# A layer norm's scale moved into VectorE's product and its bias into narrow matmuls, in place of ScalarE's affine step

## The chip, the cores and the metric

The kernel runs on one core of one Trainium2 chip. The metric is the device time of one execution in microseconds (us), and the median of several executions is compared.

## What is computed

Two sequences of 1024 tokens with 128 channels go through a recurrent mixing layer and a norm, then through six layers of local attention (16 heads of 64, windows of 32) and feed-forward, and a last norm. The change lies in the feed-forward, whose hidden width is 341, twice (a and gate). All of it is fp32. Cut to what matters:

```python
def ffn_layer(x, g, bln, W1, b1, W2, b2):
    mu = x.mean(-1, keepdims=True)
    var = ((x - mu) ** 2).mean(-1, keepdims=True)
    xn = (x - mu) / jnp.sqrt(var + 1e-05) * g + bln
    hg = xn @ W1 + b1
    a, gate = jnp.split(hg, 2, -1)
    return a * jax.nn.gelu(gate, approximate=False) @ W2 + b2
for i in range(DEPTH):
    x = attn_layer(shift_tokens(x), Wqkv[i], q_scale[i], k_scale[i], Wo[i]) + x
    x = ffn_layer(shift_tokens(x), ln_g[i], ln_b[i], W1[i], b1[i], W2[i], b2[i]) + x
```

## The kernel before

The first 320 us or so are the mixing layer, which the change does not touch. After it comes the stream: 96 blocks of 128 tokens, 16 blocks to a layer, one after the other through all six layers. `x` is kept with its channels on the partitions and the tokens along the free axis, and every stage of a block is a function of the block's number `n`. The feed-forward stages work on a pair of blocks, 256 tokens, numbered `m`; a layer has eight pairs (`BLOCK_PAIRS`).

The order on each engine is written by hand. Each engine has a `turn`, a list of stages with lags, and `stream` runs it once for each `n`: `at(2, turn_k)` means that turn `n` does `turn_k` for block `n - 2`, and `pair(5, norm_x)` does `norm_x` for a pair in every other turn, once its second block is five turns back. So a pair of turns makes one period. The engines meet in semaphores only, one for each kind of step (`Signal`), and `after(n)` is the count that tells that block or pair `n` has it.

The attention part of a block: TensorE projects q and k in four products of 512 columns (`project_qk`, L1370) and v in two (`project_v`, L1375); ScalarE squares q and k (`square`, L1603), VectorE multiplies them with the rotary tables (`rotate`, L1770) and sums the squares (`norms`, L1776), ScalarE makes the inverse norms, GpSimd adds the turned halves (L1308) and applies the norms (L1314). TensorE transposes q and k (L1383), multiplies them in small tiles (`scores`, L1418), VectorE subtracts the peak and sums (L1782 to L1798), GpSimd normalizes the probabilities (L1332) and multiplies the rotary tables by the gains (L1297, `gains`, which `rotate` of the block waits for). VectorE turns the probabilities in blocks of 32 (`turn_p`, L1804), the SP queue places them and shifted values with DMAs, and TensorE makes the outputs in small tiles (`outputs`, L1443).

The feed-forward part of a pair: `project_o` (L1460, eight products of 256 columns into `FF_BANK`) waits for `o_T` and for `x_ready` of the pair before. `add_attention` on VectorE (L1809) adds `x` and writes `xm`; `centres` (L1467) subtracts the mean with a matmul, ScalarE squares (L1650), `variances` (L1471) takes the mean of the squares, and `inverse_sigma` on ScalarE (L1655, L1657) makes `rstd`, spread over all partitions. VectorE's `norm_x` (L1814) multiplies the centred tile by `rstd` into `xn`, and ScalarE's `affine` (L1663) makes `xn_T` of it with the scale and the bias of the layer, one number a channel and so one a partition. TensorE's `up` (L1477) makes the gate columns and then the a columns from `xn_T` in three parts of 128, 128 and 85 (`FF_PARTS`). ScalarE's `gelu` (L1670) adds b1's gate part, VectorE's `gated` (L1822) adds b1's a part and multiplies, `down` (L1501) is the second product, and `add_ffn` (L1843) writes the new `x` and sets `x_ready`.

The piece of TensorE's turn in which the change puts its matmuls:

```python
            at(0, project_qk, 3)
            at(0, project_v, 0)
            pair(4, project_o, 0)
            pair(4, project_o, 1)
            at(3, outputs, 0)
```

After the last turn the stages that are left stand in a list of their own, with the last norm and the stores of the result between them. The weights of a layer (2.4 MB) are loaded one layer ahead by the SP queue, behind the DMAs of the seventh block of the layer in work.

## Time and profile before

| what | value |
|---|---|
| median of 3 runs | 1926.08 us (1924.15 to 1927.91) |
| profiled execution, span from its first to its last instruction | 1924.9 us |
| profiled execution, its own time | not on the page; the runs' median is 1.2 us above its span |
| instructions in the span | 72907 |
| busy share of the span: PE, PEld, DVE, ACT, POOL | 91%, 62%, 81%, 59%, 65% |
| TensorE's granted clock, mean | 0.958 of full speed |
| stream | from about 320 us to the end, 96 blocks |

PE is TensorE's matmuls, PEld its weight loads, DVE is VectorE, ACT is ScalarE, POOL is GpSimd. In the profile an fp32 matmul of the program appears as two records, each with a weight load of its own; the transposes appear as one. A start that follows the one before by less than that one's duration is a pipelined start, so what an instruction costs in a row of its kind is the distance of starts. In the timelines "x16" merges sixteen records, and what stands in brackets is idle time before them and what ended it. The rows that the prediction uses stand in a section of their own below.

### The profile page before, as it was taken

How to read it: one execution, taken by the hardware profiler on the slowest of the kernel's cores; microseconds unless marked ns; L12 is line 12 of the kernel's file. 1: busy time of each engine (PE TensorE's matmuls, PEld its weight loads, DVE VectorE, ACT ScalarE, POOL GpSimd, SP SyncE). 2: the span in 40 equal slices, each digit the busy share in tenths (PEclk: the TensorE clock that was granted, in tenths of full speed). 3: DMA queues.
4: the chain of work that ended last, by engine and by line, in shares of the span. 5: the costliest groups of instructions: out<-in, count | busy, mean ns of one | idle time of the engine just before them, and what ended most of it. 6: DMA issues, size and time to landing. Idle time of an engine off the chain costs nothing.

```text
span 1924.9 us, 72907 instructions
## 1 busy us (share of the span) xinstructions
PE 1751.1 (91%) x31158; PEld 1185.3 (62%) x31158; DVE 1550.0 (81%) x2150; ACT 1138.0 (59%) x2221; POOL 1259.8 (65%) x981
## 2 busy tenths in 40 slices
PE   7577876899999989999899999899998999999985
PEld 2144553466666666667666767666666676666663
DVE  6599957788888878888888888788887888888853
ACT  5523223557676747676667676667675667676742
POOL 3476743777777767777667777677776777777730
PEclk9699977999999989999999999999998999999986
DMA  4534201222222232222322222322223222222220
GB/s 97 127 53 51 29 3 70 58 67 70 69 73 68 72 104 79 63 75 70 112 66 79 69 73 83 103 62 77 69 72 109 69 68 79 63 76 67 70 61 26
DMA packets 68257, 137.27 MB, mean 71 GB/s; under 512 B 17952, under 2 KB 23520, under 8 KB 66912
## 3 DMA queue, kind: packets, MB, share of 16 engines
q1 hardware_dynamic: 67936, 132.62, 27.0%
q8 instruction: 246, 4.03, 0.9%
q14 instruction: 75, 0.61, 0.1%
HBM read 29.79 MB, written 2.10 MB: 17 GB/s over the span
## 4 chain that ended last, share of the span: by engine, by line
PE 40%; DVE 22%; issue 11%; POOL 9%; DMA 7%; ACT 4%; SPq 2%; DVEq 0%; ACTq 0%; POOLq 0%
PE bank L1460 9%; PE bank L1370 6%; PE bank L1443 6%; POOL rot L1308 5%; DMA v_shift<-v_tok 5%; DVE rot L1770 5%; PE bank L1418 5%; PE bank L1501 3%; PE bank L1375 3%; PE bank L1477 3%; DVE total L1796 2%; DVE rnorm L1776 2%; POOL probs L1332 2%; DVE probs L1789 2%; DMA p_T<-p_blocks 1%
## 5 line engine op out<-in xcount | busy, mean ns | idle before, releaser
L1770 DVE TENSOR_TENSOR rot<-bank,gains 128x1024 f32<-128x1024 f32 x384 | 462.3, 1206 | 158.8 <-ACT squares L1603 142.8
L1314 POOL TENSOR_TENSOR rot<-rot,rnorm 128x1024 f32<-128x1024 f32 x192 | 361.0, 1901 | 319.3 <-ACT rnorm L1613 317.1
L1308 POOL TENSOR_TENSOR rot<-rot 128x512 f32<-128x512 f32 x384 | 480.6, 1274 | 6.9 <-DVE rot L1770 6.9
L1370 PE MATMUL bank<-wqkv,x 128*128 128x512 f32 x768 | 404.9, 612 | 10.5 <-issue 5.0
L1603 ACT ACTIVATE squares<-bank 128x512 f32<-128x512 f32 x384 | 232.8, 606 | 256.5 <-PE bank L1370 255.9
L1332 POOL TENSOR_TENSOR probs<-probs,total 128x1024 f32<-128x1024 f32 x96 | 182.7, 1903 | 125.3 <-DVE total L1798 125.3
L1644 ACT ACTIVATE o_T<-bank 128x512 f32<-128x512 f32 x192 | 104.2, 598 | 254.2 <-PE bank L1443 254.2
L1776 DVE TENSOR_REDUCE rnorm<-squares 128x16 f32<-128x1024 f32 x192 | 233.0, 1214 | 2.8
L1443 PE MATMUL bank<-p_T,v_shift 64*64 64x32 f32 x6144 | 194.7, 223 | 26.6 <-DMA p_T<-p_blocks 21.9
L1443 PEld LDWEIGHTS bank<-p_T,v_shift 64*64 64x64 f32 x6144 | 169.2, 138 | 79.1 <-issue 49.6
L1383 PEld LDWEIGHTS bank<-st_ident,rot 128*128 128x128 f32 x1536 | 179.9, 143 | 59.9 <-issue 53.6
L1375 PE MATMUL bank<-wqkv,x 128*128 128x512 f32 x384 | 206.6, 621 | 2.7 <-DVE rot L1770 2.7
L1443 PE MATMUL bank<-p_T,v_tok 64*64 64x32 f32 x6144 | 193.3, 222 | 4.4 <-issue 4.4
L1383 PE MATMUL bank<-st_ident,rot 128*128 128x128 f32 x1536 | 194.0, 275 | 0.0
L1460 PE MATMUL bank<-o_T,wo 128*128 128x256 f32 x768 | 176.9, 384 | 0.0
L1443 PEld LDWEIGHTS bank<-p_T,v_tok 64*64 64x64 f32 x6144 | 170.5, 139 | 5.5 <-issue 5.4
L1477 PE MATMUL bank<-xn_T,w 128*128 128x256 f32 (+1 forms) x576 | 164.5, 395 | 9.2 <-ACT gate_T L1670 2.2
L1460 PEld LDWEIGHTS bank<-o_T,wo 128*128 128x128 f32 x768 | 146.4, 192 | 42.9 <-issue 22.4
L1418 PE MATMUL bank<-k_T,q_T 64*32 64x64 f32 x12288 | 161.8, 225 | 11.8 <-issue 10.3
L1418 PEld LDWEIGHTS bank<-k_T,q_T 64*32 64x32 f32 x12288 | 140.8, 105 | 39.2 <-issue 33.1
L1477 PEld LDWEIGHTS bank<-xn_T,w 128*128 128x128 f32 (+1 forms) x576 | 97.7, 182 | 99.2 <-DVE ff_T L1822 45.5
L1370 PEld LDWEIGHTS bank<-wqkv,x 128*128 128x128 f32 x768 | 131.6, 191 | 39.1 <-issue 16.2
(196 smaller groups left out, 2849.2 us busy)
## 6 DMA issues: line engine op xcount, KB each, us to landing
p_T<-p_blocks SPq DMA_DIRECT2D x768, 64.0 KB
v_shift<-v_tok SPq DMA_DIRECT2D x96, 384.0 KB, 3.5
v_shift<-v_tok SPq DMA_DIRECT2D x96, 128.0 KB, 3.4
wqkv<-in_wqkv SPq DMA_DIRECT2D x6, 1536.0 KB, 8.0
v_rep_sb<-v_by_step SPq DMA_DIRECT2D x32, 128.0 KB
v_rep<-v_by_step SPq DMA_DIRECT2D x32, 128.0 KB
wo<-in_wo SPq DMA_DIRECT2D x6, 512.0 KB, 8.6
w<-in_w SPq DMA_DIRECT2D x6, 341.0 KB, 8.8
```

The source lines that it names most:

```text
L1308: nc.gpsimd.tensor_tensor(out=out, in0=out, in1=by_head(turned[:, part])[:, :, frm], op=ALU.add).then_inc(rot_added.sem, 1)
L1314: nc.gpsimd.tensor_tensor(out=by_head(qk[u][:, half]), in0=by_head(qk[u][:, half]), in1=rnorm[u][:, AH * i:AH * (i + 1)].unsqueeze(2).to_b ...
L1370: nc.tensor.matmul(QK_BANKS[i][:, :], shifted_tokens(x, n, P), layer_cols(wqkv, n, 3 * INNER, 512 * i, 512), start=True, stop=True).then_i ...
L1375: nc.tensor.matmul(V_BANKS[i][:, :], shifted_tokens(x, n, P), layer_cols(wqkv, n, 3 * INNER, 2 * INNER + 512 * i, 512), start=True, stop=T ...
L1383: mm = nc.tensor.transpose(outs[i // 4][:, P * (i % 4):P * (i % 4 + 1)], source[:, P * i:P * (i + 1)], ident[:, :])
L1418: mm = nc.tensor.matmul(s_banks(n)[p][at:at + WINDOW, 2 * WINDOW * a_:2 * WINDOW * (a_ + 1)], q_T[rows, a_, at:at + WINDOW], k_T[rows, a_, ...
L1443: mm = nc.tensor.matmul(o_banks(n)[g][DH * p:DH * (p + 1), at:at + WINDOW], v[rows, DH * head:DH * (head + 1)], p_T[n % 2][rows, turn_, he ...
L1460: mm = nc.tensor.matmul(ff_bank(m)[:, 0:PT], layer_cols(wo, n, INNER, C * i, C), o_T[:, i, :], start=(i == 0), stop=(i == PAIRS - 1))
L1477: mm = nc.tensor.matmul(ff_bank(m)[0:size, PT * j:PT * (j + 1)], layer_cols(w1, PAIR * m, 2 * FF, at + f0, size), xn_T[:, :], start=True, ...
L1603: nc.scalar.activation(squares[:, 512 * i:512 * (i + 1)], QK_BANKS[i][:, :], ACT.Square).then_inc(squared.sem, 1)
L1770: nc.vector.tensor_tensor(both, src.unsqueeze(1).to_broadcast([P, 2, 8, DH]), pair_of_gains.unsqueeze(2).to_broadcast([P, 2, 8, DH]), ALU. ...
L1776: nc.vector.reduce_sum(rnorm[n % 2][:, AH * h:AH * (h + 1)], by_head(squares[:, INNER * h:INNER * (h + 1)]), AX).then_inc(ss_made.sem, 1)
```

## The change

`norm_x` on VectorE becomes one instruction with two multiplications, (centred x scale) x rstd, and writes `xn_T` itself. The bias of the norm goes around the large product: once a layer, `shift_up` on TensorE multiplies the layer's W1, six column parts of it, with the column of the norm's bias, into six unused columns of `FF_BANK`, ahead of `project_o` of the layer's first pair. `shift_b1` on VectorE adds b1 to them with four small instructions ahead of that pair's `xm` and writes `b1_shifted`, which `gelu` and `gated` use in place of b1. ScalarE's `affine` is gone, and with it the tile `xn` and its semaphore. The waits that went with it are moved: the first logarithm of `inverse_sigma` waits for `xnT_made` of the pair before, and `norm_x` waits for the a product of the pair before, which has read `xn_T`.

```diff
+        def shift_up(m):
+
+            layer = m // BLOCK_PAIRS
+            for i, (f0, size) in enumerate(FF_PARTS):
+                for half in range(2):
+                    nc.tensor.matmul(FF_BANK[0:size, PT + len(FF_PARTS) * half + i:PT + len(FF_PARTS) * half + i + 1],
+                                     layer_cols(w1, PAIR * m, 2 * FF, FF * half + f0, size),
+                                     norm_gb[:, layer + DEPTH:layer + DEPTH + 1], start=True, stop=True)
+
         def project_o(m, h):
...
+            if h == 0 and m % BLOCK_PAIRS == 0:
+                shift_up(m)
             for i in range(PAIRS // 2 * h, PAIRS // 2 * (h + 1)):
...
         def inverse_sigma(m):
             act.wait_ge(var_product.sem, var_product.after(m))
-            act.wait_ge(x_normed.sem, x_normed.after(m - 1))
+            act.wait_ge(xnT_made.sem, xnT_made.after(m - 1))
...
-        def affine(m):
-            act.wait_ge(x_normed.sem, x_normed.after(m))
-            act.wait_ge(a_product.sem, a_product.after(m - 1))
-            layer = m // BLOCK_PAIRS
-            nc.scalar.activation(xn_T[:, :], xn[:, :], ACT.Identity, scale=norm_gb[:, layer:layer + 1],
-                                 bias=norm_gb[:, layer + DEPTH:layer + DEPTH + 1]).then_inc(xnT_made.sem, 1)
-
         def gelu(m, i):
-            size, col = FF_PARTS[i][1], (m // BLOCK_PAIRS) * 2 * len(FF_PARTS) + len(FF_PARTS) + i
+            size, layer, col = FF_PARTS[i][1], m // BLOCK_PAIRS, len(FF_PARTS) + i
+            act.wait_ge(b1_made.sem, layer + 1)
...
-                                 bias=b1[0:size, col:col + 1]).then_inc(gate_made.sem, 1)
+                                 bias=b1_shifted[layer % 2][0:size, col:col + 1]).then_inc(gate_made.sem, 1)
...
+        def shift_b1(layer):
+
+            cols = 2 * len(FF_PARTS)
+            for size, parts in ((P, (0, 1)), (FF_PARTS[-1][1], (2,))):
+                for half in range(2):
+                    part = slice(len(FF_PARTS) * half + parts[0], len(FF_PARTS) * half + parts[-1] + 1)
+                    add = nc.vector.tensor_tensor(b1_shifted[layer % 2][0:size, part], FF_BANK[0:size, PT:PT + cols][:, part],
+                                                  b1[0:size, cols * layer:cols * (layer + 1)][:, part], ALU.add)
+            add.then_inc(b1_made.sem, 1)
+
         def add_attention(m):
             dve.wait_ge(y_product.sem, y_product.after(m))
+            if m % BLOCK_PAIRS == 0:
+                shift_b1(m // BLOCK_PAIRS)
...
         def norm_x(m):
             dve.wait_ge(rstd_made.sem, rstd_made.after(m))
-            dve.wait_ge(xnT_made.sem, xnT_made.after(m - 1))
-            nc.vector.tensor_tensor(xn[:, :], ff_bank(m)[:, 0:PT], rstd[:, :], ALU.mult).then_inc(x_normed.sem, 1)
+            dve.wait_ge(a_product.sem, a_product.after(m - 1))
+            layer = m // BLOCK_PAIRS
+            nc.vector.scalar_tensor_tensor(out=xn_T[:, :], in0=ff_bank(m)[:, 0:PT], scalar=norm_gb[:, layer:layer + 1], in1=rstd[:, :],
+                                           op0=ALU.mult, op1=ALU.mult).then_inc(xnT_made.sem, 1)
 
         def gated(m, i):
...
+            dve.wait_ge(b1_made.sem, layer + 1)
...
-                                           scalar=b1[0:size, col:col + 1], in1=gate_T[0:size, i, :],
+                                           scalar=b1_shifted[layer % 2][0:size, i:i + 1], in1=gate_T[0:size, i, :],
```

TensorE in the turn in which the first pair of the second layer has its `project_o` (`w` is W1 or W2, `bank` a PSUM bank). Before:

```order
L1370 MATMUL bank<-wqkv,x 128x512
L1501 MATMUL bank<-ff_T,w_0 128x256 x3
L1370 MATMUL bank<-wqkv,x 128x512
L1375 MATMUL bank<-wqkv,x 128x512
L1460 MATMUL bank<-o_T,wo 128x256 x8
L1443 MATMUL bank<-p_T,v_shift 64x32 x4
L1443 MATMUL bank<-p_T,v_tok 64x32 x4
```

And now:

```order
L1372 MATMUL bank<-wqkv,x 128x512
L1514 MATMUL bank<-ff_T,w_0 128x256 x3
L1372 MATMUL bank<-wqkv,x 128x512
L1377 MATMUL bank<-wqkv,x 128x512
L1455 MATMUL bank<-norm_gb,w_1 128x1 x4
L1455 MATMUL bank<-norm_gb,w_1 85x1 x2
L1473 MATMUL bank<-o_T,wo 128x256 x8
L1445 MATMUL bank<-p_T,v_shift 64x32 x4
L1445 MATMUL bank<-p_T,v_tok 64x32 x4
```

The six narrow matmuls stand between `project_v` and `project_o`; the rest is as before, with other line numbers.

VectorE at the first pair of the first layer, from the last `rot` of one turn to the second of the next. Before:

```order
L1770 TENSOR_TENSOR rot<-bank,gains 128x2x512
L1809 TENSOR_TENSOR xm<-bank,x 64x256 x2
L1776 TENSOR_REDUCE rnorm<-squares 128x16
L1804 STREAM_TRANSPOSE p_blocks<-probs 128x1024
L1770 TENSOR_TENSOR rot<-bank,gains 128x2x512
L1814 TENSOR_TENSOR xn<-bank,rstd 128x256
L1770 TENSOR_TENSOR rot<-bank,gains 128x2x512
```

And now (`b_shifted` is `b1_shifted`):

```order
L1773 TENSOR_TENSOR rot<-bank,gains 128x2x512
L1815 TENSOR_TENSOR b_shifted<-bank,b 128x2 x2
L1815 TENSOR_TENSOR b_shifted<-bank,b 85x1 x2
L1824 TENSOR_TENSOR xm<-bank,x 64x256 x2
L1779 TENSOR_REDUCE rnorm<-squares 128x16
L1807 STREAM_TRANSPOSE p_blocks<-probs 128x1024
L1773 TENSOR_TENSOR rot<-bank,gains 128x2x512
L1830 SCALAR_TENSOR_TENSOR xn_T<-bank,norm_gb,rstd 128x256
L1773 TENSOR_TENSOR rot<-bank,gains 128x2x512
```

The four small adds stand ahead of `xm`, and the product that wrote `xn` is a SCALAR_TENSOR_TENSOR that writes `xn_T`.

## Rows read from the trace of the kernel before

**Rows 1.** The page's head and its part 1 (busy us, share, instructions)
```profile
span 1924.9 us, 72907 instructions
...
PE 1751.1 (91%) x31158; PEld 1185.3 (62%) x31158; DVE 1550.0 (81%) x2150; ACT 1138.0 (59%) x2221; POOL 1259.8 (65%) x981
```

**Rows 2.** Windows of three pairs: us; busy PE, PEld, DVE, ACT, POOL; clock; DMA
```profile
1103.22:1134.24 31.02, 30.91 (x617) 21.45 (x611) 26.85 (x35) 21.17 (x41) 22.70 (x17) 1.00 0.27 70
1009.70:1040.90 31.20, 31.09 (x613) 21.78 (x610) 27.16 (x35) 21.17 (x41) 23.02 (x19) 1.00 0.26 70
1196.70:1235.40 38.70, 33.28 (x618) 23.39 (x611) 26.97 (x35) 21.54 (x41) 22.85 (x18) 0.91 0.43 128
```

**Rows 3.** Chain of waits, 1095 to 1165: start us, us, what
```profile
1107.72 0.65 ACT squares L1603
...
1109.53 0.41 DVE xn L1814
...
1117.22 1.06 POOL probs L1332
```

**Rows 4.** Timeline of PE, 1100 to 1136: start us, us, work
```profile
1103.22 0.70 PE L1467 MATMUL bank<-xm,centring 128*128 128x256 f32 x2
...
1104.62 1.91 PE L1383 MATMUL bank<-st_ident,rot 128*128 128x128 f32 x16
1106.36 1.02 PE L1370 MATMUL bank<-wqkv,x 128*128 128x512 f32 x2
...
1110.47 1.13 PE L1370 MATMUL bank<-wqkv,x 128*128 128x512 f32 x2
1111.43 1.03 PE L1477 MATMUL bank<-xn_T,w 128*128 128x256 f32 x4
...
1124.55 1.13 PE L1370 MATMUL bank<-wqkv,x 128*128 128x512 f32 x2
1125.51 1.46 PE L1501 MATMUL bank<-ff_T,w 128*128 128x256 f32 x6
...
1128.55 3.69 PE L1460 MATMUL bank<-o_T,wo 128*128 128x256 f32 x16
1132.17 0.32 PE L1443 MATMUL bank<-p_T,v_shift 64*64 64x32 f32 x8
...
1134.24 0.70 PE L1467 MATMUL bank<-xm,centring 128*128 128x256 f32 x2
```

**Rows 5.** Timeline of DVE, the same stretch
```profile
1102.18 0.86 DVE L1809 TENSOR_TENSOR xm<-bank,x 64x256 f32<-64x256 f32 x2
...
1133.32 0.86 DVE L1809 TENSOR_TENSOR xm<-bank,x 64x256 f32<-64x256 f32 x2
```

**Rows 6.** Part 5 (busy us, mean ns | idle before), weight loads
```profile
L1460 PEld LDWEIGHTS bank<-o_T,wo 128*128 128x128 f32 x768 | 146.4, 192 | 42.9 <-issue 22.4
```

**Rows 7.** Timeline of PE, first pair of the first layer
```profile
395.70 1.02 PE L1467 MATMUL bank<-xm,centring 128*128 128x256 f32 x2 [1.34 <-DVE xm L1809]
```

**Rows 8.** Groups by line and form, DVE and ACT, 300 to 1900
```profile
L1789 DVE TENSOR_TENSOR probs<-bank,peak 128x512 f32<-128x512 f32 x192 | 122.7, 680 | 0.0
...
L1822 DVE SCALAR_TENSOR_TENSOR ff_T<-bank,b,gate_T 128x256 f32<-128x256 f32 x94 | 41.2, 480 | 71.7 <-PE bank L1477 71.7
...
L1814 DVE TENSOR_TENSOR xn<-bank,rstd 128x256 f32<-128x256 f32 x48 | 19.9, 415 | 8.0 <-ACT rstd L1657 8.0
...
L1663 ACT ACTIVATE xn_T<-xn,norm_gb 128x256 f32<-128x256 f32 x48 | 28.1, 586 | 1.0 <-DVE xn L1814 1.0
```

**Rows 9.** Timeline of ACT, 1100 to 1136
```profile
1111.69 0.60 ACT L1603 ACTIVATE squares<-bank 128x512 f32<-128x512 f32 x1 [0.73 <-PE bank L1370]
```

**Rows 10.** Waits of the weight loads, 400 to 1800: us in total, times, longest
```profile
PEld bank L1477 <- ACT xn_T L1663: 9.7, 38, 0.4
```

**Rows 11.** Timelines of ACT and PE in the tail
```profile
1896.35 0.58 ACT L1663 ACTIVATE xn_T<-xn,norm_gb 128x256 f32<-128x256 f32 x1
...
1896.60 1.80 PE L1501 MATMUL bank<-ff_T,w 128*128 128x256 f32 x6 [2.66 <-DVE ff_T L1822]
```

More of the change, by code:

```diff
@@ L1125, in build_stream @@
     xm = sb("xm", (P, B, T + 1))
-    cent_sq, rstd, xn, xn_T = (sb(n, (P, PT)) for n in ("cent_sq", "rstd", "xn", "xn_T"))
+    cent_sq, rstd, xn_T = (sb(n, (P, PT)) for n in ("cent_sq", "rstd", "xn_T"))
+    b1_shifted = two("b1_shifted", (P, 2 * len(FF_PARTS)))
     gate_T, ff_T = sb("gate_T", (P, len(FF_PARTS), PT)), sb("ff_T", (P, len(FF_PARTS), PT))
@@ L1149, in build_stream @@
     cent_squared, var_product, var_log, rstd_made = sig("cent_squared"), sig("st_var_product"), sig("var_log"), sig("rstd_made")
-    x_normed, xnT_made = sig("x_normed"), sig("xnT_made")
+    xnT_made = sig("xnT_made")
+    b1_made = sig("b1_made", credit=0)
     gate_product, gate_made, a_product = sig("up_gate_product", per=2), sig("gate_made", per=3), sig("up_a_product", per=2)
@@ L1592, in scalar @@
         for s in (squared, above_floor, rnorm_log, rnorm_made, v_read, qT_made, kT_made, exp_made, oT_made,
-                  cent_squared, var_log, rstd_made, xnT_made, gate_made):
+                  cent_squared, var_log, rstd_made, gate_made):
             act.sem_inc(s.sem, s.credit * s.per)
@@ L1692, in turn @@
             at(1, inverse_norms)
-            pair(5, affine)
             at(0, square, 2)
@@ L1716, in scalar @@
         inverse_sigma(m - 2)
-        affine(m - 2)
         read_q(LAST)
@@ L1727, in scalar @@
         inverse_sigma(m - 1)
-        affine(m - 1)
         read_o(LAST - 1)
@@ L1736, in scalar @@
         final_inverse(0, 0, 12)
-        affine(m)
         gelu_full(m)
@@ L1749, in vector @@
             nc.vector.memset(tile, 0.0).then_inc(cleared.sem, 1)
-        for s in (x_ready, rotated, ss_made, peak_made, shifted, total_made, p_turned, xm_made, x_normed, ff_made):
+        for s in (x_ready, rotated, ss_made, peak_made, shifted, total_made, p_turned, xm_made, xnT_made, ff_made):
             dve.sem_inc(s.sem, s.credit * s.per)
@@ L1812, in norm_x @@
             dve.wait_ge(rstd_made.sem, rstd_made.after(m))
-            dve.wait_ge(xnT_made.sem, xnT_made.after(m - 1))
-            nc.vector.tensor_tensor(xn[:, :], ff_bank(m)[:, 0:PT], rstd[:, :], ALU.mult).then_inc(x_normed.sem, 1)
+            dve.wait_ge(a_product.sem, a_product.after(m - 1))
+            layer = m // BLOCK_PAIRS
+            nc.vector.scalar_tensor_tensor(out=xn_T[:, :], in0=ff_bank(m)[:, 0:PT], scalar=norm_gb[:, layer:layer + 1], in1=rstd[:, :],
+                                           op0=ALU.mult, op1=ALU.mult).then_inc(xnT_made.sem, 1)
         def gated(m, i):
-            size, col = FF_PARTS[i][1], (m // BLOCK_PAIRS) * 2 * len(FF_PARTS) + i
+            size, layer = FF_PARTS[i][1], m // BLOCK_PAIRS
+            dve.wait_ge(b1_made.sem, layer + 1)
             dve.wait_ge(a_product.sem, a_product.after(m, 1 + i // 2))
```

## The prediction

> **What bounds the kernel now.** I read the page first: TensorE is busy 91% of the span of 1924.9 us [rows 1]. That share is a mean over stages, so next came the windows [rows 2]: a steady pair of blocks takes 31.02 us, another 31.20 us, with TensorE busy in all but 0.1 us of it and its clock granted in full (1.00, the level of 2.4 GHz), and a pair in which a layer's weights are loaded takes 38.70 us, where TensorE stands still for 5.4 us. Then the chain of waits over one pair [rows 3]. It goes through ScalarE's squares, VectorE's stretch from `rot` over `xn` to `total`, and GpSimd's `probs` and `rot`, before it comes back to TensorE. So two cycles run side by side: TensorE's own work, and one that passes through VectorE and GpSimd. Which of them ends last decides what each edit is worth.
>
> The timelines of that pair show how close they are. TensorE [rows 4]: `project_o` (from 1128.55, 3.62 us long) is followed at once by `outputs` (1132.17), and `centres` starts at 1134.24. VectorE [rows 5]: `xm`, which `centres` waits for, ends at 1133.32 + 0.86 = 1134.18, only 0.06 us before. One pair earlier it ends at 1103.04 and `centres` starts at 1103.22, 0.18 us later. Taken in the same way, 19 of 44 pairs have the small distance (0.05 to 0.08 us: VectorE ends last) and 25 the large one (0.15 to 0.28 us: TensorE ends last).
>
> **The narrow matmuls (six a layer).** Where the order rows have eight `project_o` matmuls, the trace has sixteen records, so an fp32 matmul runs as two, and six make twelve: eight with 128 weight columns, four with 85. With one moving column each, the weight load sets their time. The nearest row is the transposes [rows 4]: 16 records from 1104.62 to 1106.36, each with a load of 128 columns of its own, 0.109 us apart. Twelve, with the narrower ones scaled, are 0.109 x (8 + 4 x 85/128) = 1.2 us a layer. Lower bound: `outputs` runs 128 records in 2.07 us on four quadrants, 0.065 us for a 64-column load and its matmul in a quadrant, so 12 x 0.065 = 0.8 us. Upper bound: 0.192 us, what a 128-column load lasts alone [rows 6], 2.3 us. I take 1.2, since the transposes have the same loads in the same close order. The Trainium skill (TensorE: Matmul & The Clock Gate, LDWEIGHTS) gives a load's time as its columns / 1.2 in ns; the twelve would be 1.1 us by it, an estimate, and the sum 0.5 us smaller.
>
> All of it stands on TensorE between `project_v` and `project_o`, where there is no hole, and `outputs`, the reads by ScalarE behind it and so both cycles come after it. Five layers pay in full, 6.0 us. The first pays less: there TensorE waited 1.34 us for `xm` [rows 7], since VectorE was late with its own work. The product for `xm` comes 1.2 us later, still inside that work, and only what VectorE itself adds ahead of `xm` is left, some 0.3 us. Sum: **+6.3 us** (bounds 4.3 and 11.8).
>
> **VectorE's product.** A TENSOR_TENSOR of 0.415 us becomes a SCALAR_TENSOR_TENSOR of 128x256 with an operand in PSUM, and that costs 0.480 us in `gated` [rows 8]: 0.065 us x 48 = 3.1 us if all of it were on the path. It stands in the stretch of [rows 3], whose lateness comes back through GpSimd's `gains` to VectorE's next `rot`. In the 19 close pairs it shows; in the 25 others it fits into the 0.1 us by which TensorE is later: 19 x 0.065 = **+1.2 us** (0 to 3.1).
>
> **VectorE's four small adds a layer.** A tensor_tensor takes 0.415 us at 256 columns and 0.680 at 512 [rows 8]; drawn down to one or two columns that is 0.15 us, so four are at most 0.6 us. Behind them in the queue stand `xm`, the second `rnorm` and the next `p_blocks`. The product that they wait for now ends 1.2 us later, just as VectorE is done with its last `rot`. From there 0.1 + 0.6 + 0.86 us to the end of `xm` are 1.56 us, while TensorE is in `outputs` for 2.07 us: **0 us** (0.6 x 6 = 3.6 us if that cover were gone). `p_blocks` comes 0.6 us later where all of TensorE comes 1.2 us later.
>
> **ScalarE's affine step.** 48 x 0.586 = 28.1 us of busy time go [rows 8]. In the pair it is followed by 0.73 us of idle time until TensorE's product for the third square [rows 9], so that square starts no earlier: **0 us**. `xn_T` itself is ready earlier, straight from VectorE. The weight loads of the gate product did wait for it, 9.7 us in 38 times [rows 10], but its matmuls not visibly: from `project_qk` 2 to the gate product are 0.96 us, and exactly as much from `project_qk` 2 to `down` in the other half [rows 4], whose `ff_T` had been ready for over 1 us. So 0 here too (at best -9.7 us).
>
> **Waits.** The gelu and `gated` now also wait for `b1_made`, which is set a block ahead of them; the first logarithm and the product now wait for things of the pair before that were done some 10 us earlier: 0. Behind the gelu on ScalarE stand the reads of `o_T`, and so TensorE, but what it waits for is not later than before. The queues of SP and GpSimd issue what they did.
>
> **The tail.** For the last pair the affine step ran from 1896.35 to 1896.93, while TensorE was in `down` of the pair before, from 1896.60 to 1898.40 [rows 11]. Taking it out gives nothing. The longer product stands ahead of the last part of `ff_T`, for which that `down` had waited: +0.1 us.
>
> **Sum:** 6.3 + 1.2 + 0.1 = +7.6 us, on the profiled span 1932.5 us. The page gives no other time for that execution; the median of the three runs, 1926.08 us, is 1.2 us above the span, so I add to the median: **1933.7 us**, 0.4% slower. A difference of 0.2% (3.9 us) is about what a measurement of this kernel can tell from none.
>
> **Rivals.**
> 1. *VectorE becomes the bound.* Every pair pays 0.065 us and every layer the adds: 6.3 + 3.1 + 3.6 = +13.0 us, 1939.1 us. For it: the 19 close pairs. Against: the 0.1 us in hand in the other 25, and the 0.5 us over the adds. Chance 0.14.
> 2. *The narrow matmuls and their loads take turns.* Each record then costs a load of 0.192 us [rows 6] and a short matmul, for which I take 0.2 us (eight of `outputs` end within 0.32 us [rows 4]): 12 x 6 x 0.39 = 28 us, with the rest +29 us, 1955 us. Against: the sixteen records of `project_o` take 3.62 us, 0.226 each, and would take 0.4 if the loads were not beside them. Chance 0.03. By the Trainium skill (TensorE: Matmul & The Clock Gate, The mechanism) a load overlaps a running matmul only when it goes to another row group, and these all take the full height, so that section speaks for this rival; here the trace does not agree with it, by the 0.226 us.
> 3. *The narrow matmuls are absorbed,* in the stalls of the weight loads (38.70 against 31.1 us [rows 2]) and in the 0.2 us that `project_o` is slower than its columns. Then 1.3 us are left: 1927.4 us, no change. Against: the stalls come two blocks behind these matmuls, and the transfers that cause them are released by TensorE's `outputs`, so they move with it. Chance 0.08.
> 4. *TensorE gets back the wait for `xn_T`.* 7.6 - 9.7 = -2.1 us: 1924.0 us, no change. For it: [rows 10]. Against: the 0.96 us in both halves. Chance 0.05.
> 5. *Faster, because ScalarE was on the path.* This decides from the point at which ScalarE has no idle time ahead of the third square: then a pair gains the affine step's own time, 28.1 us in all, less 7.6: 1905.6 us. For it: the chain passes through ScalarE's squares. Against: the 0.73 us [rows 9], and no piece of the chain in this pair is the affine step. Chance 0.05, with the cases in which a part of it joins rival 4.
>
> **How the numbers follow.** The forecast has the 0.65 that is left. Slower by over 0.2%: the forecast and rivals 1 and 2, 0.82, less 0.02 for a forecast that a measurement places lower: 0.80. Within 0.2%: rivals 3 and 4 and that 0.02: 0.15. Faster: 0.05. The range leaves out rivals 2, 4 and 5, 0.13. Its foot is rival 3, 1927.0; its head, 1941.0, is rival 1 with a third of the way from 6.3 to 11.8 for the loads.
>
> **What would show it.** Right: narrow matmuls 0.1 us apart and 1.2 us more from `project_v` to `project_o` in the first pair of layers two to six; the product at 0.48 us; ScalarE 28 us less busy and idle for as much longer ahead of `squares`; `xm` ready some 0.5 us before `centres` in a layer's first pair; other pairs at 31.0 to 31.2 us. Wrong: ordinary pairs above 31.3 us (rival 1), 0.3 us or more from one narrow matmul to the next (rival 2), pairs with stalls shorter than 38 us (rival 3), ordinary pairs under 31.0 us (rivals 4 and 5).

## The result, and the profile after

The changed kernel takes 1936.31 us (median of 8 runs, 1928.77 to 1941.79), the kernel before 1923.42 us in the same session (8 runs, 1918.60 to 1929.32). The ratio is 1.0057 with a 95% interval of 1.0037 to 1.0078: slower by 11.0 us, between 7.1 and 15.0. The two medians alone are 12.9 us apart, which lies inside the same interval. The forecast was +7.6 us and slower. Differences below are ratios to the kernel before, turned into us with 1923.42; the quotient of two medians can be another one, by up to 3.4 us. One of the 12 executions of run 10 took 2077.15 us, at a granted clock of 0.82 where the others had 0.95 to 0.96, and is left out of its ratio.

The profiled execution of the change was the fastest of its eight, 1928.77 us, with a span of 1926.8. So its page shows where single pieces went, but not the whole difference. The head and part 1 of its page, against [rows 1]:

```profile
span 1926.8 us, 73122 instructions
...
PE 1752.9 (91%) x31230; PEld 1190.3 (62%) x31230; DVE 1553.7 (81%) x2174; ACT 1114.2 (58%) x2173; POOL 1260.3 (65%) x981
```

TensorE has 72 records more (6 x 12), VectorE 24 more, ScalarE 48 fewer. ScalarE is busy for 23.8 us less. The forecast's 28.1 us were the affine step alone; its other groups differ between the two executions as well. What became of that time is in part 5 of the same page, in the row of the squares:

```profile
L1616 ACT ACTIVATE squares<-bank 128x512 f32<-128x512 f32 x384 | 232.6, 606 | 273.6 <-PE bank L1372 273.0
```

On the page of the kernel before, the same group has 256.5 us idle ahead of it. 17.1 of the 23.8 us have turned into waiting for TensorE. In the pair itself, the 0.73 us of [rows 9] are now 1.40 (ScalarE's timeline, 1104 to 1128):

```profile
1109.37 0.60 ACT L1616 ACTIVATE squares<-bank 128x512 f32<-128x512 f32 x1 [1.40 <-PE bank L1372]
```

The windows of three pairs from `centres` to `centres`, with the columns of [rows 2]: an ordinary one, the first of a layer, and one in which a layer's weights are loaded.

```profile
1100.72:1131.98 31.26, 31.09 (x615) 21.76 (x611) 27.23 (x35) 20.67 (x40) 22.98 (x19) 1.00 0.27 70
1131.97:1164.19 32.22, 32.05 (x629) 22.69 (x623) 27.92 (x39) 20.68 (x40) 23.90 (x18) 1.00 0.26 68
1195.38:1235.88 40.50, 34.29 (x617) 23.98 (x611) 27.05 (x35) 21.01 (x40) 22.89 (x18) 0.92 0.41 123
```

From `centres` to `centres`, the first pairs of layers two to six took 31.01, 31.06, 31.27, 31.17 and 31.91 us before, and take 32.64, 32.22, 32.21, 32.20 and 32.21 now: 1.0 us more on average. The shortest ordinary pair is 31.07 us against 31.02, while the mean of the ordinary pairs under 31.45 us (neither the first of a layer nor one in which weights are loaded, and without the tail) is 31.15 against 31.16. The four pairs in which weights are loaded took 38.37 to 40.57 us before and 37.56 to 40.50 now, with no direction in them.

TensorE's timeline where layer one turns over, 385 to 400. The matmuls of `project_v` are followed by the narrow ones and these by `project_o`; it answers to [rows 7]:

```profile
385.38 1.12 PE L1377 MATMUL bank<-wqkv,x 128*128 128x512 f32 x2
386.35 1.25 PE L1455 MATMUL bank<-norm_gb,w 128*128 128x1 f32 x12
387.46 3.70 PE L1473 MATMUL bank<-o_T,wo 128*128 128x256 f32 x16
...
393.56 0.70 PE L1480 MATMUL bank<-xm,centring 128*128 128x256 f32 x2 [0.41 <-DVE xm L1824]
```

Twelve records from 386.35 to 387.46: 1.11 us, 0.093 us each. It is 1.11 and 1.12 us in layers two and three, and 1.19 us (0.099 each) in layers four to six. And the idle time ahead of `centres` fell from 1.34 to 0.41 us, so in this pair most of the added time was taken out of a wait that was there already, as the forecast had it.

The group of the weight loads at that line (count: shortest/median/longest ns, first to last start; forms), then VectorE's groups of the small adds and of the product:

```profile
L1455 PEld LDWEIGHTS bank<-norm_gb,w x72: 155/190/192, 385.9 to 1678.8; 128*128 128x128 f32 x48, 128*85 128x85 f32 x24
```

```profile
L1815 DVE TENSOR_TENSOR b_shifted<-bank,b x24: 143/146/160, 392.4 to 1682.8; 128x2 f32<-128x2 f32 x12, 85x1 f32<-85x1 f32 x12
L1830 DVE SCALAR_TENSOR_TENSOR xn_T<-bank,norm_gb,rstd x48: 450/475/483, 399.9 to 1896.3; 128x256 f32<-128x256 f32 x48
```

A load lasts 190 ns by its own record, yet a load and its matmul come every 93 ns, so these loads overlap each other as well, as far as their records tell. The product is 475 ns (forecast 480, before 415) and an add 146 ns (forecast 150).

VectorE's and TensorE's timelines, 1158 to 1176, in the first pair of layer four. They answer to [rows 4, 5]:

```profile
1161.06 1.16 DVE L1773 TENSOR_TENSOR rot<-bank,gains 128x1024 f32<-128x1024 f32 x1
1162.30 0.35 DVE L1815 TENSOR_TENSOR b_shifted<-bank,b 128x2 f32<-128x2 f32 x4
1162.57 0.87 DVE L1824 TENSOR_TENSOR xm<-bank,x 64x256 f32<-64x256 f32 x2
...
1170.50 0.47 DVE L1830 SCALAR_TENSOR_TENSOR xn_T<-bank,norm_gb,rstd 128x256 f32<-128x256 f32 x1
```

```profile
1158.56 3.70 PE L1473 MATMUL bank<-o_T,wo 128*128 128x256 f32 x16
...
1164.19 0.70 PE L1480 MATMUL bank<-xm,centring 128*128 128x256 f32 x2
```

The four adds overlap and delay `xm` by 0.27 us, not 0.6. `xm` ends at 1163.44 and `centres` starts at 1164.19, with 0.75 us in hand. Forecast were 0.5.

So far each step looks as forecast. One distance does not. In the half of a pair in which `down` is issued, the forecast put the new wait of `gated` at nothing. Here is TensorE's timeline of the kernel before, 1114 to 1133, and that of the change, 1104 to 1128, from the second `project_qk` of the turn to the last a product (`up_a_tail`, 85 weight columns). That product waits for `ff_T`, which VectorE makes with two `gated` steps in a row:

```profile
1120.97 1.02 PE L1370 MATMUL bank<-wqkv,x 128*128 128x512 f32 x2
1122.10 0.66 PE L1477 MATMUL bank<-xn_T,w 128*85 128x256 f32 x2
```

```profile
1118.65 1.02 PE L1372 MATMUL bank<-wqkv,x 128*128 128x512 f32 x2
1119.84 0.66 PE L1490 MATMUL bank<-xn_T,w 128*85 128x256 f32 x2 [0.17 <-DVE ff_T L1840]
```

1.13 us have become 1.19, and TensorE is now shown as waiting 0.17 us for `ff_T`. It waited there before as well: `project_qk` ends at 1120.97 + 1.02 = 1121.99 and the product starts 0.11 us later, too little for the timeline to show. So VectorE's `ff_T` came last at this place already, and anything that delays `gated` reaches TensorE. Over 45 pairs the median went from 1.132 to 1.187 us: 0.055 us a pair, 2.5 us in the span if every pair became longer by as much.

### The profile page after: what moved, and what is told of

Same layout as the page of the kernel before. It is cut to its first block and busy times, and to the rows that moved or that the text cites. A ratio compares the mean times of both kernels' runs of the same rounds, so it can differ in the third digit from the quotient of the medians.

```text
span 1926.8 us, 73122 instructions
## 1 busy us (share of the span) xinstructions
PE 1752.9 (91%) x31230; PEld 1190.3 (62%) x31230; DVE 1553.7 (81%) x2174; ACT 1114.2 (58%) x2173; POOL 1260.3 (65%) x981
```

## The experiments

Two theories went in for the 3.4 us between forecast and result, although the interval of the result (7.1 to 15.0) does not force such a gap. By the first, it is the wait of `gated` for `b1_made`, which is always met but stands as a fourth wait ahead of a step with three. By the second, each part costs somewhat more than forecast: the product in every pair, or the narrow matmuls do, by what they do to the clock or to the weight loads behind them. Each run gives the median of its own kernel; the ratio is to the kernel before, timed on the same chip in the same session (medians 1924.73 to 1925.33 us there).

**1. The wait for `b1_made` once a layer** (against the changed kernel):

```diff
             size, layer = FF_PARTS[i][1], m // BLOCK_PAIRS
-            dve.wait_ge(b1_made.sem, layer + 1)
+            if i == 0 and m % BLOCK_PAIRS == 0:
+                dve.wait_ge(b1_made.sem, layer + 1)
             dve.wait_ge(a_product.sem, a_product.after(m, 1 + i // 2))
```

and the same in the gelu, with `act`.

> The change, with the wait for b1_made taken once a layer (first pair, first part of gelu and of gated) in place of six times a pair. What it computes is unchanged. Seen in the trace of the change: from the second project_qk of a turn to the last a product, TensorE needs 1.19 us where before it needed 1.13, in every pair, and VectorE's ff_T starts 1.11 us after the a product in place of 1.06. Theory A (a fourth wait ahead of gated delays it by 0.05 to 0.06 us each pair, on TensorE's path): the distance returns to 1.13 us and the time is 2 to 3 us below the change. Theory B (the distance comes from the new operand tile or from the state of the run, not from the wait): 1.19 us stays, no difference to the change.

Measured: 1934.11 us (6 runs), ratio 1.0051 (1.0034 to 1.0068), so +9.8 us; and the distance is back at 1.132 us. With the wait gone from all but the layer's first step, the longer distance is gone. The ratio agrees with a gain of 1.2 us over the change, and with none, since the intervals lie over each other.

**2. The change without the shift of b1.** The call of `shift_up`, the adds and the waits for `b1_made` go, and the gelu and `gated` take `b1` as before:

```diff
-            if h == 0 and m % BLOCK_PAIRS == 0:
-                shift_up(m)
...
-            if m % BLOCK_PAIRS == 0:
-                shift_b1(m // BLOCK_PAIRS)
...
-            dve.wait_ge(b1_made.sem, layer + 1)
```

> The change without its narrow matmuls, small adds and b1_made: the norm's bias is left out of the result, b1 is used as it is. It leaves VectorE's longer product and the missing affine step. Theory of the prediction: slower than before by 1.2 us (0 to 3.1), pairs in which VectorE ends last at 31.08 us in place of 31.02, the first pair of a layer like any other (31.1 to 31.3 us, against 32.2 in the change). Rival (ScalarE's freed time is worth something): faster than before by 3 us or more. Rival (the narrow matmuls cost more than their 1.1 us, for instance in later stalls): the change less this one is well over 9 us.

Measured: 1927.84 us (12 runs), ratio 1.0013 (0.9998 to 1.0029), so +2.5 us (-0.4 to 5.6). Its first pairs take 31.1 to 31.4 us but for one of 32.18, and the distance is 1.132 us. What is left of the change in it is the product and the missing affine step. Against run 1, the narrow matmuls and the adds are worth 1.0051 - 1.0013, or 7.3 us, with some 4 us of uncertainty.

**3. The narrow matmuls twice** (against the changed kernel):

```diff
-            for i, (f0, size) in enumerate(FF_PARTS):
+            for i, (f0, size) in list(enumerate(FF_PARTS)) * 2:
                 for half in range(2):
```

> The change with the six narrow matmuls of a layer made twice (the same columns written again). Theory: twelve more records 0.1 us apart, so the first pair of layers two to six takes 33.3 us in place of 32.2, 5 to 6 us in all over the change. Rival (they are taken up by the stalls behind the weight loads): the first pairs grow, the stalled pairs (37.6 to 40.5 us) shrink by as much, no difference to the change.

Measured: 1950.22 us (4 runs), ratio 1.0137 (1.0112 to 1.0161), so +26.4 us, and 15.4 more than the change. Doubling a cost of 5.6 to 7.3 us should add as much again, not twice as much. TensorE's timeline, 1690 to 1706, and the windows on and behind the narrow matmuls of the sixth layer show a part of it:

```profile
1694.83 2.45 PE L1455 MATMUL bank<-norm_gb,w 128*128 128x1 f32 x24
1697.14 5.39 PE L1473 MATMUL bank<-o_T,wo 128*128 128x256 f32 x16
```

```profile
1694.80:1697.90 3.10, 3.10 (x29) 2.99 (x28) 3.07 (x3) 0.98 (x2) 1.66 (x2) 1.00 0.00 0
1697.90:1701.30 3.40, 3.40 (x10) 2.69 (x9) 1.56 (x3) 0.00 (x0) 2.81 (x2) 0.50 0.00 0
```

`project_o` takes 5.39 us in place of 3.70, because the granted clock right behind the 24 narrow records is 0.50, the level of 1.2 GHz. The same happens in layer five (3.41 us from 1435.1), and in no other. In those two layers the first pairs take 35.32 and 35.60 us, in the other three 34.11, 33.41 and 33.41 (35.60 and 34.11 hold a pause of 0.35 and of 0.61 us on TensorE besides, of the kind that the end of the next section describes). Set against 33.41 us, the two clock drops come to 1.9 and 1.8 us. Behind the twelve narrow records of the change every such window has a clock of 1.00:

```profile
1158.50:1162.00 3.50, 3.50 (x19) 3.00 (x18) 3.46 (x4) 0.00 (x0) 1.90 (x2) 1.00 0.02 5
```

**4. The kernel before, with `gated` waiting for its product alone:**

```diff
             dve.wait_ge(a_product.sem, a_product.after(m, 1 + i // 2))
-            dve.wait_ge(gate_made.sem, gate_made.after(m, i + 1))
-            dve.wait_ge(y2_product.sem, y2_product.after(m - 1))
```

> The kernel before, with gated on VectorE waiting for the a product alone; the two other waits are implied by it, since TensorE makes the a product only after the gate tile is made and after the down product of the pair before. Nothing else differs. Theory A (a wait ahead of gated costs some 0.05 us on TensorE's path): from the second project_qk to the last a product 1.02 to 1.08 us in place of 1.13, pairs in which TensorE ends last shorter by as much, 2 to 5 us faster than before. Theory B (waits that are already met cost nothing): 1.13 us, no difference.

Measured: 1926.97 us (12 runs), ratio 1.0004 (0.9987 to 1.0022); the distance is 1.133 us. One wait or three ahead of `gated` is the same, in the distance and, within 4 us, in the time.

**5. The kernel before, without the affine step;** its result lacks the norm's scale and bias, and the product writes `xn_T` itself:

```diff
-            nc.vector.tensor_tensor(xn[:, :], ff_bank(m)[:, 0:PT], rstd[:, :], ALU.mult).then_inc(x_normed.sem, 1)
+            nc.vector.tensor_tensor(xn_T[:, :], ff_bank(m)[:, 0:PT], rstd[:, :], ALU.mult).then_inc(xnT_made.sem, 1)
...
-        affine(m - 2)
```

> The kernel before without ScalarE's affine step: VectorE's product (a TENSOR_TENSOR, as before) writes xn_T itself, and the scale and the bias of the norm are left out of the result. Theory (ScalarE is not on the path): no difference to before, within 0.1%; ScalarE 28 us less busy, idle for as much longer. Rival (part of the freed time, or of TensorE's weight loads that waited for xn_T, comes back): 3 to 10 us faster.

Measured: 1926.73 us (11 runs), ratio 1.0001 (0.9987 to 1.0016). On its page the idle time ahead of `squares` rises from 256.5 to 277.9 us. 28.1 us of busy time gone are worth nothing, within 3 us either way; so rival 4 (9.7 us to be gained) and rival 5 (28.1 us) are out.

**6. The scale alone moved into the product,** with the affine step kept for the bias, the kernel before otherwise:

```diff
-            nc.vector.tensor_tensor(xn[:, :], ff_bank(m)[:, 0:PT], rstd[:, :], ALU.mult).then_inc(x_normed.sem, 1)
+            layer = m // BLOCK_PAIRS
+            nc.vector.scalar_tensor_tensor(out=xn[:, :], in0=ff_bank(m)[:, 0:PT], scalar=norm_gb[:, layer:layer + 1], in1=rstd[:, :],
+                                           op0=ALU.mult, op1=ALU.mult).then_inc(x_normed.sem, 1)
```

> The kernel before with the norm's scale in VectorE's product (SCALAR_TENSOR_TENSOR) and the affine step kept for the bias. Same result. Theory: the product takes 0.475 us in place of 0.415, the pairs in which VectorE ends last take 31.08 us in place of 31.02, about 1 us slower than before (0 to 3), too little to be told from none in the times. Rival (VectorE's extra comes back in every pair): all ordinary pairs 0.06 us longer, 3 us slower.

Measured: 1928.76 us (10 runs), ratio 1.0017 (1.0004 to 1.0030), so +3.3 us (0.8 to 5.8). The shortest pair is 31.07 us, as in the change; the mean of the ordinary pairs is 31.155 us, as before (31.160). The time lies nearer to the product in every pair (3.1 us) than to 19 of 44 (1.2 us), but the interval holds both. The trace lies between: of its 44 pairs, 27 have the small distance from `xm` to `centres` that the forecast counted 19 times in the kernel before (25 of 44 in run 2). 27 x 0.065 = 1.8 us.

**7. The kernel before, with a fourth wait ahead of `gated`,** for a semaphore that has always been raised by then:

```diff
+            dve.wait_ge(gains_made.sem, gains_made.after(2 * m))
             dve.wait_ge(a_product.sem, a_product.after(m, 1 + i // 2))
```

> The kernel before with a fourth wait ahead of gated on VectorE, for a count that was reached long before. Same result. Theory: the distance from the second project_qk to the last a product is 1.19 us in place of 1.13 in every pair; where TensorE ends last the pair is 0.06 us longer, so 1 to 3 us slower than before. Rival (the distance in the change came from something else): 1.13 us, no difference.

Measured: 1931.24 us (12 runs), ratio 1.0030 (1.0016 to 1.0044), so +5.8 us (3.1 to 8.5). The distance is 1.187 us, the same as that of the change (TensorE's timeline):

```profile
1119.24 1.02 PE L1370 MATMUL bank<-wqkv,x 128*128 128x512 f32 x2
1120.43 0.66 PE L1477 MATMUL bank<-xn_T,w 128*85 128x256 f32 x2 [0.17 <-DVE ff_T L1823]
```

No data and no work differ here. A wait that is met on arrival costs time, and the row that names `ff_T` as what TensorE waits for comes from it. How it reaches the pairs is less simple. Windows of the same two neighbouring pairs, in the kernel before and then here:

```profile
978.69:1009.72 31.03, 30.92 (x617) 21.34 (x611) 26.82 (x35) 21.17 (x41) 22.65 (x17) 1.00 0.27 71
1009.72:1040.92 31.20, 31.09 (x610) 21.78 (x611) 27.16 (x35) 21.17 (x41) 23.02 (x19) 1.00 0.26 70
```

```profile
975.63:1006.65 31.02, 30.86 (x616) 21.34 (x610) 26.84 (x35) 21.17 (x41) 22.69 (x17) 1.00 0.27 70
1006.65:1037.89 31.24, 31.07 (x612) 21.73 (x611) 27.19 (x35) 21.17 (x41) 23.10 (x19) 1.00 0.26 70
```

The distance is longer in both, but the short pair is not: there VectorE's `xm` ends last, and it takes up TensorE's 0.055 us. The long pair, in which TensorE ends last, is. Over the trace the mean of the ordinary pairs under 31.45 us rises from 31.160 to 31.179 us only. So 2.5 us is an upper bound for what the distance gives, the pairs of this one execution show 1 us of it, and where the rest of the measured 3.1 to 8.5 us arises is not shown.

**8. Three wide matmuls ahead of the narrow ones** (against the changed kernel). They have 256 moving columns each, and should take 1.28 us in all and leave the clock alone:

```diff
+            for i in range(3):
+                nc.tensor.matmul(FF_BANK[:, PT:2 * PT], layer_cols(wo, PAIR * m, INNER, C * i, C), o_T[:, i, :], start=True, stop=True)
             for i, (f0, size) in enumerate(FF_PARTS):
```

> The change with three more matmuls of 128x256 ahead of the six narrow ones in a layer's first pair (their columns are overwritten, the result is the same). They take six records of 0.213 us, 1.28 us, about what the second set of narrow matmuls took (1.19 us a layer). That one came out 14 us above the change where 6 us were added, and its trace shows 3.4 us at the granted clock of 1.2 GHz right behind the twenty-four narrow records of two layers. Theory A (narrow matmuls leave TensorE's array idle enough for the clock to fall): with wide ones the clock stays at 2.4 GHz behind them and the time is 6 to 8 us above the change, so 5 us or more below the doubled one. Theory B (whatever is put there costs more than its own time, through the buffers and queues behind it): as slow as the doubled one, 1950 us.

Measured: 1950.02 us (5 runs), ratio 1.0114 (1.0090 to 1.0137), so +21.9 us, 11 more than the change where 6 x 1.28 = 7.7 were added. The clock stays at full speed behind them:

```profile
1698.00:1701.40 3.40, 3.40 (x91) 2.86 (x92) 1.77 (x7) 0.00 (x0) 3.40 (x3) 1.00 0.00 0
```

This run was to tell whether the excess of run 3 is the clock's, and it doesn't. It is about as slow as run 3 within the two intervals. Its profile has first pairs of 33.56 to 34.69 us, whose sum is 8.9 us above that of the change, where five times 1.28 are 6.4. It also has 12 other pairs over 31.5 us, where the change has 8. In the first pairs the 2.5 us beyond the work are pauses: 34.68 and 34.69 us hold one of 1.15 and one of 1.18 us each. So an excess can come without any drop of the clock. How much of run 3's is the clock stays open; its two drops come to 3.7 us in the profiled execution, of which `project_o` has 1.7 each.

**9. The narrow matmuls alone,** added to the kernel before, their result unused:

```diff
+            if h == 0 and m % BLOCK_PAIRS == 0:
+                shift_up(m)
             for i in range(PAIRS // 2 * h, PAIRS // 2 * (h + 1)):
```

> The kernel before with the six narrow matmuls a layer added to TensorE and used by nobody; result, waits, product and affine step as before. Theory (their own time is what they cost): the first pairs of layers two to six take 32.1 to 32.2 us in place of 31.1, 5 to 6 us slower than before in all, more than half of what the whole change costs (11 us measured). Rival (they cost more than that, since TensorE's instructions behind them are fetched late, or the clock falls behind them): 8 us or more, with more pairs that hold a pause of 1 us behind an instruction fetch, or with granted clock of 1.2 GHz behind them.

Measured: 1931.86 us (8 runs), ratio 1.0029 (1.0015 to 1.0043), so +5.6 us (2.9 to 8.3). Its first pairs take 33.24, 32.42, 32.15, 32.15 and 32.34 us, 5.9 us more in all than before, or 4.9 without a pause of 0.95 us in the first. The distance is 1.132 us, and `norm_x`, the affine step and the waits are those of the kernel before. So the narrow matmuls alone are half of the measured difference.

**10. The kernel before, without waits elsewhere** that others imply: one ahead of `outputs`, and three ahead of `rot`, whose first step of a block then has two in place of four:

```diff
-                pe.wait_ge(v_read.sem, v_read.after(n))
...
-                dve.wait_ge(q_turned.sem, q_turned.after(n - 2))
             if i == 2:
-                dve.wait_ge(k_turned.sem, k_turned.after(n - 2))
-            if i % 2 == 0:
                 dve.wait_ge(rot_added.sem, rot_added.after(n - 1, 2 * (i // 2 + 1)))
```

> The kernel before with waits taken out that others imply: rotate's for q_turned and k_turned, its rot_added where gains_made implies it, and v_read ahead of outputs, so that the first rotate has two waits in place of four and outputs three in place of four. Same result. Theory A (every wait above three costs about 0.055 us where its engine is on the path): rotate starts 0.03 us or so behind gains in place of 0.09, and the time falls by 1 to 3 us below before. Theory B (only what was added to gated costs something): the same time and distances as before.

Measured: 1927.10 us (12 runs, the ratio from 11), ratio 1.0009 (0.9996 to 1.0022). Nothing is to be had by fewer waits here either, although a step went from four to two. In its trace `rot` starts 0.10 us behind the `gains` that it waits for, where it was 0.09 before and 0.03 were expected. So what a fourth wait costs ahead of `gated` is not a price of every step with four.

**11. Three more waits, all met,** six in all ahead of `gated` (the kernel before):

```diff
+            dve.wait_ge(gains_made.sem, gains_made.after(2 * m))
+            dve.wait_ge(squared.sem, squared.after(2 * m))
+            dve.wait_ge(rot_added.sem, rot_added.after(2 * m))
             dve.wait_ge(a_product.sem, a_product.after(m, 1 + i // 2))
```

> The kernel before with three more waits ahead of gated (six in all), for counts reached long before. Same result. With one more, the distance to the last a product rose from 1.13 to 1.19 us and the time by 5.8 us (3.1 to 8.5), more than 0.055 us in each of 45 pairs can give (2.5 us). Theory A (each further wait is a step of 0.055 us): 1.30 us, and 5 to 9 us slower than before. Theory B (waits go in pairs, or a threshold is passed once): 1.19 to 1.24 us, and 3 to 6 us slower. If it comes out at under 3 us, the 5.8 us of the one wait was for the most part scatter of the runs.

Measured: 1937.95 us (6 runs), ratio 1.0062 (1.0044 to 1.0080), so +12 us. The distance is 1.397 us over the pairs (TensorE's timeline, 1126 to 1132 in one of them):

```profile
1127.98 1.02 PE L1370 MATMUL bank<-wqkv,x 128*128 128x512 f32 x2
1129.37 0.66 PE L1477 MATMUL bank<-xn_T,w 128*85 128x256 f32 x2 [0.38 <-DVE ff_T L1825]
```

0.265 us more x 45 pairs = 11.9 us, about the measured time. The pairs of the trace agree with that in part only. These are the windows of the same two as in run 7:

```profile
984.04:1015.25 31.21, 30.84 (x617) 21.55 (x611) 27.04 (x35) 21.17 (x41) 22.89 (x18) 1.00 0.27 70
1015.25:1046.50 31.25, 30.87 (x617) 21.63 (x611) 26.88 (x35) 21.17 (x41) 22.73 (x17) 1.00 0.26 70
```

Now the short pair is longer too. But the mean of the ordinary ones rises by 0.10 us (31.260 against 31.160), which makes 4.4 us over 44 pairs. That the waits cost time is clear of the noise here; that they cost it by the distance alone is not shown.

**12. The narrow matmuls four times,** as run 3 with `* 4`.

> The change with the narrow matmuls made four times (twenty-four, forty-eight records, some 4.6 us in a layer's first pair). Same result. Theory A (narrow matmuls let the granted clock fall): behind most of the six places the clock is 1.2 GHz for a stretch, the first pairs take 36 us and another 2 us for each stretch, 30 us or more above the change. Theory B (the two stretches behind the doubled ones were chance): full clock behind all six, first pairs at 35.7 us, 18 to 22 us above the change.

Measured: 1976.72 us (3 runs), ratio 1.0266 (1.0247 to 1.0285), so +51 us. The granted clock now falls in each of the six layers. TensorE's timeline at the fifth (1440 to 1470), then windows of 7 us at the first, the second and the fifth, which begin within the 48 narrow records:

```profile
1449.60 6.93 PE L1455 MATMUL bank<-norm_gb,w 128*128 128x1 f32 x48
1456.40 6.58 PE L1473 MATMUL bank<-o_T,wo 128*128 128x256 f32 x16
```

```profile
391.00:398.00 7.00, 7.00 (x42) 6.24 (x42) 4.25 (x5) 0.62 (x1) 4.58 (x4) 0.76 0.01 2
650.00:657.00 7.00, 7.00 (x29) 6.35 (x30) 1.64 (x3) 0.00 (x0) 5.35 (x5) 0.52 0.00 0
1452.00:1459.00 7.00, 7.00 (x31) 6.55 (x31) 2.25 (x3) 0.00 (x0) 5.37 (x5) 0.50 0.01 2
```

At the fifth, the 48 records last 6.8 us, 0.142 each and not 0.093, and `project_o` takes 6.58 us. So the clock does fall behind 48 of these records, in layers two, four and five already among them, and behind the twelve of the change it does not.

## Why the prediction was right, and where it was off

Direction and range held, and the largest term was right by its mechanism. +7.6 us lies within the measured 7.1 to 15.0, at its low end; two terms were too small. That the time of 1936.31 us is only 2.6 us above the forecast 1933.7 is in part luck: the kernel before came out 2.7 us below the median of 1926.08 to which the forecast was added.

- **Narrow matmuls, +6.3 us:** right. The distance of starts was put at 0.109 us from the transposes, scaled to 0.097 over the twelve, and is 0.093 to 0.099; 1.2 us a layer are 1.11 to 1.19. The first layer paid little, since 0.93 of its 1.34 us of waiting went. Alone they measure +5.6 us (run 9). By the Trainium skill (TensorE: Matmul & The Clock Gate, LDWEIGHTS) a load takes its columns / 1.2 in ns; the estimate of 1.1 us a layer that follows fits these as well.
- **VectorE's product, +1.2 us:** perhaps too small. Its duration was right (475 ns). The share of pairs that pay was taken as fixed at 19 of 44, but a later VectorE makes more pairs close: 25 and 27 in the traces of runs 2 and 6, which makes 1.6 to 1.8 us. Their times say +2.5 us (-0.4 to 5.6) and +3.3 us (0.8 to 5.8), nearer to the bound of 3.1 for all pairs. But their ordinary pairs are no longer on average than before (31.158 and 31.155 us against 31.160), and the shortest by 0.05 us. So a size above 1.2 us is possible and not shown.
- **Small adds, 0:** right. They delay `xm` by 0.27 us, inside the cover, of which 0.75 us are left.
- **ScalarE's affine step, 0, and `xn_T`'s weight loads, 0:** right. Run 5 takes the step out of the kernel before and finds 1.0001; its time turns into waiting for `squares`.
- **"Waits ... 0":** the step that failed. It asked only whether `b1_made` is raised in time, and priced a wait that is met at nothing. Ahead of `gated`, which already had three waits, a fourth puts TensorE's last a product 0.055 us later in every pair. Run 1 takes it off (with that of the gelu), and run 7 puts a wait like it into the kernel before, with nothing else changed. By the distance that is 2.5 us at most; run 7 timed it at 5.8 (3.1 to 8.5). The place to look was TensorE's 0.11 us of waiting for `ff_T` in the kernel before, since any lateness of `gated` shows there.

With the terms as timed, the sum is 5.6 + 2.5 to 3.3 + 5.8 = 13.9 to 14.7 us, and 10.6 to 11.4 with 2.5 us for the wait; 11.0 were measured. By what the pairs of the traces show, it is less: 5.1 for the narrow matmuls (the five first pairs), 1.2 to 1.8 for the product and 1 to 2.5 for the wait, 7.3 to 9.4 in all. Each term has an interval of 3 us or so either way, so that the second sum meets the 11.0 is no proof of its parts.

Of the rivals, the first (+13.0 us) came nearest to the measured time, nearer than the forecast, but its mechanism did not come: the adds cost nothing where it had 3.6 us, and its sign, ordinary pairs above 31.3 us, is absent. It came near because something else was in their place, the wait that no rival had. The second, turns taken by narrow matmuls and their loads, needed 0.39 us from record to record; there are 0.093 to 0.099, with loads of 0.190. The section of the Trainium skill that spoke for it (TensorE: Matmul & The Clock Gate, The mechanism: a load overlaps a running matmul only in another row group) does not hold for these full-height matmuls. The third, absorption in the stalls, is out by run 9 and by the 1.0 us in the first pairs; the four pairs with weights loaded sum to 157.8 us before and 157.5 now, where 5 us should have gone. One of them is 37.56 us with no absorption, so the sign that the forecast named for it, under 38 us, was no test: such pairs scatter from 38.37 to 40.57 us in the kernel before alone.

What stays open: the size of the product's share, where in the span the wait's 5.8 us arise, and why runs 3 and 8 are 15 and 11 us slower than the change where 5.6 to 7.7 us of work were added. Part of the scatter that hides this can be seen in every trace, a pause of about 1 us among small matmuls, for which the profile names no releaser (the kernel before, TensorE's timeline, 374 to 412):

```profile
405.76 0.43 PE L1418 MATMUL bank<-k_T,q_T 64*32 64x64 f32 x24 [1.39 <-issue]
```

In the traces of the kernel before and of the change, a transfer of the instruction queue begins 0.8 to 1.8 us ahead of 14 of the 15 such pauses of 0.8 us or more. But one begins about every 5.5 us in any case, so this is only seen together; no run tested it. No version beats the kernel before: the two with fewer waits and the one without the affine step lie within 0.1% of it.

## What to carry to other kernels

A wait can cost time even when its semaphore is always raised in time: ahead of a step whose result another engine waits for last, a fourth cost 0.055 us a pair here and three more 0.265 us, while elsewhere going from four to two gave nothing. So look first for such a step, and take a wait for something set once a layer at the first step of the layer and at no other. Busy time taken from an engine that idles for another is worth nothing, as 28.1 us of ScalarE's were. And price a row of narrow matmuls at the distance at which their overlapping loads start (0.093 to 0.099 us), and look at the granted clock behind it.

## What the runs showed of the hardware that was not expected

- **Waits that are met on arrival are not always free, and not linear.** From the second `project_qk` to the last a product, with two `gated` steps between: 1.13 us with one or three waits ahead of `gated`, 1.187 with four, 1.397 with six. Ahead of `rot`, two in place of four changed nothing (run 10).
- **Loads overlap loads.** Weight loads recorded at 190 ns with 128 columns follow each other, each with its matmul, every 93 to 99 ns.
- **The clock falls behind bursts of one-column matmuls, though TensorE is shown as busy throughout.** Behind 1.1 us of them it stayed at 2.4 GHz in all layers of the profiled executions; behind 2.4 us it fell to 1.2 GHz in two layers of six; with 48 records (4.7 us where the clock held) it fell in all six.
